# Forgetting attention: reciprocal roots on GpSimd for two units at a time, the output product in mid-slot, one spreading transfer for both heads

## What is computed

```python
q, k, v = x @ Wq, silu_conv(x @ Wk), silu_conv(x @ Wv)      # 16 heads of 64, conv of 4 taps
q = q / sqrt(mean(q**2, head) + 1e-6) * qnw                 # k likewise, with knw
cum = cumsum(log_sigmoid(x @ Wf + bf))
attn = softmax(causal(q @ k.T / 8 + cum[t] - cum[s]))
out = attn @ v
out = out / sqrt(mean(out**2, head) + 1e-6) * onw * silu(x @ Wg)
return out @ Wo
```

## Time and profile before

| | us |
|---|---|
| median of 3 runs (lowest, highest) | 2411.89 (2408.7, 2413.06) |
| the profiled execution | 2409.0 |
| its span | 2407.1 |
| `forget_units`, from the first instruction of its own to the last | 908.7 to 1955.5 |

### The profile page before, as it was taken

How to read it: one execution, slowest core, us unless ns; L and a number is a source line. 1 busy time by engine, 2 the same in 40 slices (tenths; PEclk the granted TensorE clock), 3 DMA queues, 4 the chain that set the end, 5 groups by cost and what they waited for, 6 DMA issues and landing times. The chain is left out here.

```text
span 2407.1 us, 35881 instructions
## 1 busy us (share of the span) xinstructions
PE 1917.6 (80%) x11731; PEld 872.8 (36%) x11731; DVE 1613.6 (67%) x2361; ACT 1396.5 (58%) x2254; POOL 919.5 (38%) x746
## 2 busy tenths in 40 slices
PE   5448886377775755899999999999999957599997
PEld 2113331343453422344444444444444413222222
DVE  5979995686447856778888888888886436711112
ACT  2446662333333334577777777777775533389995
POOL 0156663244014511345545555555555422700001
PEclk8779998588896977899999999999999988799999
DMA  2000000000000010111111111112111100411120
GB/s 89 0 13 0 0 0 0 1 1 1 0 1 0 1 38 24 39 58 57 57 57 57 57 57 57 56 59 57 57 57 58 46 19 18 114 40 48 46 53 36
DMA packets 66143, 86.12 MB, mean 36 GB/s; under 512 B 13344, under 2 KB 37216, under 8 KB 65888
## 3 DMA queue, kind: packets, MB, share of 16 engines
q1 hardware_dynamic: 60944, 81.37, 11.4%
q10 hardware_dynamic: 5040, 2.72, 0.4%
HBM read 72.12 MB, written 11.93 MB: 35 GB/s over the span
## 5 line engine op out<-in xcount | busy, mean ns | idle before, releaser
L2001 ACT ACTIVATE rt_p<-rt_ps_s 128x1024 f32<-128x1024 f32 x256 | 240.3, 1040 | 32.8 <-PE rt_ps_o L1946 17.4
L1634 DVE SCALAR_TENSOR_TENSOR fu_kv<-fu_ps_kv,fa_vec,fu_kv 128x511 f32<-128x511 f32 x366 | 252.6, 738 | 6.4 <-ACT fu_kv L1542 5.5
L1706 POOL TENSOR_TENSOR fu_p<-fu_p 128x768 f32<-128x768 f32 x64 | 116.7, 1823 | 260.2 <-PE fu_ps_n L1392 255.8
L1362 PE MATMUL fu_ps_s<-fu_qn,fu_kn 64*128 64x512 f32 (+3 forms) x1024 | 190.8, 470 | 7.4 <-ACT fu_p L1529 5.6
L601 POOL TENSOR_TENSOR scan_hC<-scan_h,scan_c 128x1024 f32<-128x1024 f32 x64 | 150.7, 2355 | 84.4 <-DVE scan_h L581 84.4
L1392 PE MATMUL fu_ps_n<-fu_p,fu_vt 128*64 128x512 f32 (+3 forms) x1024 | 166.0, 445 | 0.0
L526 PE MATMUL scan_ps_y<-scan_hC,w_ident 128*128 128x512 f32 x256 | 132.1, 640 | 40.9 <-POOL scan_hC L601 24.3
L581 DVE TENSOR_TENSOR_SCAN scan_h<-scan_dA,scan_ps_b 128x1024 f32<-128x1024 f32 x64 | 146.4, 2287 | 2.2
L1717 POOL TENSOR_TENSOR fu_num<-fu_num,fu_sg 128x512 f32<-128x512 f32 x64 | 81.3, 1270 | 172.3 <-DVE fu_sg L1667 172.3
L1946 PE MATMUL rt_ps_o<-rt_p,rt_va 128*32 128x512 f32 x1024 | 138.1, 611 | 10.0 <-ACT rt_p L2001 8.1
L1420 PE MATMUL fu_ps_kv<-w_XN,fa_wp 128*128 128x512 f32 x244 | 126.6, 643 | 16.7 <-DVE fu_cr L1599 15.3
(11 more groups left out here) (349 smaller groups left out, 4942.4 us busy)
## 6 DMA issues: line engine op xcount, KB each, us to landing
fu_rb<-rms_rows SPq DMA_DIRECT2D x256, 128.0 KB, 2.9
fu_ro<-rms_rows SPq DMA_DIRECT2D x128, 128.0 KB, 3.0
ra_stackq<-rope_parts SPq DMA_DIRECT2D x168, 32.0 KB
ra_stackk<-rope_parts SPq DMA_DIRECT2D x168, 32.0 KB
rope_parts<-rp_q SPq DMA_DIRECT2D x24, 128.0 KB, 2.0
rope_parts<-rp_k SPq DMA_DIRECT2D x24, 128.0 KB, 2.0
rms_rows<-fu_r SPq DMA_DIRECT2D x14, 192.0 KB, 2.1
w_X<-in_xT SPq DMA_DIRECT2D x4, 512.0 KB
```

Source lines behind the costliest of these rows:

```text
L1362: pe.matmul(sps[:, h, at:at + T - t * P], k[head(h), t * P:(t + 1) * P], q[head(h), t * P:T], start=(at == 0), stop=False)
L1634: dve.scalar_tensor_tensor(acc, projected(a, k)[:, 0:T - j], vec[:, a % GA, at:at + 1], acc, ALU.mult, ALU.add).then_inc(done, 1)
L1706: pool.tensor_tensor(tail, tail, P13[:, :, 0:3 * P], ALU.add).then_inc(s.d1, 1)
L2001: act.activation(pr[k % 2][i][:, :, :], sps[(U * n + u) % RING][:, :, :], ACT.Exp, scale=DH_B ** -0.5).then_inc(s.exp, 1)
```

## The change

WIN is 2: each second slot (i % 2 == 1) is a root slot. AHEAD is still 8, OUT is 4 (each unit's output a slot earlier; `o` is i - 5, so that odd o, with the output projection, falls into even slots, and never into a root slot). In a root slot ACT now adds epsilon for queries and keys (an Identity with bias, 64 x 512) in DVE's place, and squares; DVE adds for the output (1633 in the new numbering). The two function table loads, Ln and Exp are gone. In their place SP folds the mean squares, 4 rows of 512 for each of the three kinds, into 32 partitions x 64 (`VAR`, up to four small transfers), DVE makes a first guess of 1/sqrt by integer arithmetic on the bits (1663), and GpSimd refines it with eleven instructions on 96 x 64, each waiting for the one before (1731 to 1752), between its sums of probabilities and the gating of `fu_num`. The write of the roots to DRAM stands in the next, even slot.

The output product moves from the start of DVE's slot to behind the last tap, ahead of the last reduction. The spread is one transfer over 128 partitions in place of two over 64: `rows.rearrange("h (o t) -> h o t").broadcast_to([2, 64, T])`, with outermost count 2, then 64 with step 0.

```diff
-WIN = 4
+WIN = 2
+ROOT_SCALE = 1.8348544414191587e-20
...
-    OUT = WIN + 1
+    OUT = WIN + 2
...
+        def spread(rows):
+
+            return rows.rearrange("h (o t) -> h o t", o=1).broadcast_to([2, 64, T])
... (SP)
                         for j in range(2):
-                            for h in range(2):
-                                row = 32 * j + 2 * (u % WIN) + h
-                                sp.dma_start(RB[head(h), j, :], rows_dram[u // WIN, row:row + 1, :].broadcast_to([64, T])).then_inc(s.rb, 16)
+                            row = ROWS * j + 2 * (u % WIN)
+                            sp.dma_start(RB[:, j, :], spread(roots_dram[u // WIN, row:row + 2, :])).then_inc(s.rb, 16)
...
+                    if i % WIN == 1 and windows(i - 1) != (None, None):
...
+                        sp.wait_ge(s.msq, min(j + 1, U // WIN))
+                        sp.wait_ge(s.mso, max(j - 3, 0))
+                        for g in range(3):
+                            if g < 2 and r.start == 0:
+                                sp.dma_start(VAR[32 * g:32 * g + 32, :], MS[32 * g:32 * g + ROWS, :]).then_inc(s.fold, 16)
...
                         sp.wait_ge(s.og, u)
-                        for h in range(2):
-                            row = 64 + 16 * h + u % WIN
-                            sp.dma_start(RO[head(h), :], rows_dram[u // WIN + 2, row:row + 1, :].broadcast_to([64, T])).then_inc(s.ro, 16)
+                        row = 2 * ROWS + u % WIN
+                        sp.dma_start(RO[:, :], spread(roots_dram[u // WIN + 4, row:row + WIN + 1:WIN, :])).then_inc(s.ro, 16)
... (ACT)
+                        act.activation(MS[0:64, :], ssps[0:64, :], ACT.Identity, bias=w.eps_rms[0:64, 0:1]).then_inc(s.msq, 1)
...
-                        act.preload_act_table_set("natural_log_exp_and_others")
...
-                        act.activation(MS[r, :], MS[r, :], ACT.Ln).then_inc(s.ln, 1)
...
-                        act.activation(R[j % 2][r, :], MS[r, :], ACT.Exp, scale=-0.5).then_inc(s.r, 1)
... (DVE)
-                        dve.tensor_scalar(MS[0:64, :], ssps[0:64, :], RMS_EPS, None, ALU.add).then_inc(s.msq, 1)
...
+                        dve.tensor_scalar(ROOT[r, :].bitcast(I32), VAR[r, :].bitcast(I32), 1, 0x7fffffff, ALU.logical_shift_right, ALU.bitwise_xor).then_inc(s.bits, 1)
... (GpSimd, eleven such steps)
+                        pool.wait_ge(s.bits, j + 1)
+                        pool.tensor_scalar(y, y, ROOT_SCALE, None, ALU.mult).then_inc(s.ya, 1)
...
+                        pool.tensor_tensor(R[j % 2][r, :], y, f, ALU.mult).then_inc(s.r, 1)
```

More of the change, by code:

```diff
@@ L1288, in forget_units @@
         MS = st.sb("ms", [96, T])
-        R = [st.sb(f"r{k}", [96, T]) for k in range(2)]
+        VAR, ROOT, STEP1, STEP2 = (st.sb(n, [96, CUT]) for n in ("var", "root", "step1", "step2"))
+        R = [st.sb(f"r{k}", [96, CUT]) for k in range(2)]
         kvps, sps, mps = (st.ps(n, [P, 2, T]) for n in ("kv", "s", "m"))
         nps, ssps = st.ps("n", [P, T]), st.ps("ss", [P, T])
-        s = st.sems("set ones kvp tap t1 t2 cv th sk sv vt vc qp qc q2 k2 sa so dsq msq mso ln r rb ro put cr0 cr1 cr2 qn kn qm km "
+        s = st.sems("set ones kvp tap t1 t2 cv th sk sv vt vc qp qc q2 k2 sa so dsq msq mso fold bits ya yb yc yd y1 ye yf yg yh yi r rb ro put cr0 cr1 cr2 qn kn qm km "
                     "mx red hi ml rt rr sc ex pv d1 d2 ds n2 nc gp tg sg gated og wo x")
@@ L1612, in _ @@
                     if real(u):
-                        dve.wait_ge(s.rb, 64 * (u + 1))
+                        dve.wait_ge(s.rb, 32 * (u + 1))
                         dve.wait_ge(s.set, 9)
@@ L1713, in _ @@
                         pool.tensor_tensor(tail, tail, P13[:, :, 3 * P:T], ALU.add).then_inc(s.ds, 1)
+                    q, o = windows(i - 1) if i % WIN == 1 else (None, None)
+                    if q is not None or o is not None:
+                        j, r = (i - 1) // WIN + 3, slice(0, rows_of(q, o).stop)
+                        x, y, e, f = VAR[r, :], ROOT[r, :], STEP1[r, :], STEP2[r, :]
+                        pool.wait_ge(s.bits, j + 1)
+                        pool.tensor_scalar(y, y, ROOT_SCALE, None, ALU.mult).then_inc(s.ya, 1)
+                        pool.wait_ge(s.ya, j + 1)
+                        pool.tensor_tensor(e, y, y, ALU.mult).then_inc(s.yb, 1)
+                        pool.wait_ge(s.yb, j + 1)
+                        pool.tensor_tensor(e, e, x, ALU.mult).then_inc(s.yc, 1)
+                        pool.wait_ge(s.yc, j + 1)
+                        pool.tensor_scalar(e, e, -0.5, 1.5, ALU.mult, ALU.add).then_inc(s.yd, 1)
+                        pool.wait_ge(s.yd, j + 1)
+                        pool.tensor_tensor(y, y, e, ALU.mult).then_inc(s.y1, 1)
+                        pool.wait_ge(s.y1, j + 1)
+                        pool.tensor_tensor(e, y, y, ALU.mult).then_inc(s.ye, 1)
+                        pool.wait_ge(s.ye, j + 1)
+                        pool.tensor_tensor(e, e, x, ALU.mult).then_inc(s.yf, 1)
+                        pool.wait_ge(s.yf, j + 1)
+                        pool.tensor_scalar(f, e, 0.375, -1.25, ALU.mult, ALU.add).then_inc(s.yg, 1)
+                        pool.wait_ge(s.yg, j + 1)
+                        pool.tensor_tensor(f, f, e, ALU.mult).then_inc(s.yh, 1)
+                        pool.wait_ge(s.yh, j + 1)
+                        pool.tensor_scalar(f, f, 1.875, None, ALU.add).then_inc(s.yi, 1)
+                        pool.wait_ge(s.yi, j + 1)
+                        pool.wait_ge(s.put, 16 * max(j - 1, 0))
+                        pool.tensor_tensor(R[j % 2][r, :], y, f, ALU.mult).then_inc(s.r, 1)
                     if real(c):
```

76 lines of the change are left out of this document (39 added, 37 removed).

## The result

The changed kernel takes 3080.35 us (median of 4 runs, 3076.26 to 3084.05), the kernel before 2411.85 beside it: a ratio of 1.277, 95% interval 1.275 to 1.280, slower by 668.5 us. The forecast was 3100 in a range of 2850 to 3450. The profiled execution has a span of 3075.6. Of all executions behind this document two took far longer than the others of their kernel and are left out of every ratio, 4632.5 us in `base_ogmid_ro2` and 2540.0 in a run of the kernel before.

A forecast was written before the change was run, and what follows sets the result against it. PE bounds the kernel before (80% busy); after the change, a circle through two-engine spreads. 56 slots +668, head +21, end +4: +693 on the profiled 2409.0, forecast 3100 us, range 2850 to 3450.

The forecast's parts named there:

- The spread: two engines: RB and RO transfers, source outermost count 2: dealt out to one DMA engine per head, two of 16.
- The price: Rows on two engines at 0.086 us each: RB 11.0, RO 5.5, together 16.5 us a slot, plus 2.4 fixed.
- the fixed part: Latency of a spread transfer beyond its rows' time: 2.4 us, counted once per circle.
- The circle: Loop QN, taps, output product, SP, RO, RB, next QN: 26.8 us, 27.5 in odd slots, 3.95 less without taps.
- 56 slots: Stretch from the eighth QN to the last: 1500 us in place of 832.7, +668.
- The head: Before the eighth QN: seven intervals of 15.3 us, first QN some 4 later, one RB pushed back some 4; +21.
- The end: Last root takes three more steps but the last slot is gone: +4 us, between -5 and +15.
- What it does else: Roots, folds, GpSimd instructions, moved addition and product: all covered in a 27 us circle, priced only for the rivals.
- the first rival: New spread uses all 16 engines, landing as before in 2.9 us; product and late maxima cost: 2413 us, chance 0.06.
- the second rival: All 16 engines, and the output product runs free of GpSimd's sum: 2392 us, faster, chance 0.06.
- price none, up to 0.5 where KN meets QN: GpSimd's eleven root instructions, some 4.5 us every second slot: no cost, or up to 0.5 us.
- What would show it: Signs: fu_rb landing 11 us or more, fu_ro 7, slots of 27, QN and KN idle over 10, PE 60%, DMA 2/16.

The follow-up runs named there:

- base_ogmid_ro2: The kernel before the change with only the output product moved to mid-slot and two buffers for RO: 2418.11 us, ratio 1.0036.
- two: The changed kernel with only the old spread put back (two transfers of 64 partitions, 64 outermost on both sides): 2438.60 us, ratio 1.0119.
- two_ro2: The changed kernel with the old spread put back and two buffers for RO, so SP need not wait for the same slot's product: 2426.53 us, ratio 1.0069.
- pair: The changed kernel with 64 outermost again, each head's query and key rows in one transfer, two issues for RB: 2429.83 us, ratio 1.0083.

## Why the prediction was right

- **The spread: two engines.** Right. 0.15 of 16 engines are busy at 52 GB/s, and 4 and 8 on the source's outermost dimension give rates and times in between, with 64 on the other side. The rule of the Trainium skill (DMA: Bandwidth & Descriptors, "Why a DMA increments its semaphore by 16 and not by 1") agrees: the largest number up to 16 that divides both sizes is 2, 4 and 8 in these kernels. The smaller of the two sizes would be the same here; no run tells them apart.
- **The price.** A row was taken at 0.086, from 16 engines at work at once, and comes to 0.079 where two work alone; the fixed part was taken at 2.4 and is then 18.38 - 192 x 0.079 = 3.2. The two errors go against each other: together 18.4 (18.0 in the slot ahead) for 18.9.
- **The circle.** Right in all its pieces. From QN to the product's end, in a slot with the addition, 8.51 was forecast (1.78 + 0.72 + 1.98 + 1.19 + 1.97 + 0.87) and 8.49 is measured (1.89 + 0.72 + 1.98 + 1.19 + 1.97 + 0.74); then 0.07 for 0.07. That the parts fit to 0.02 is partly luck: QN to the instruction behind it took longer (1.89 for 1.78) and the product less (0.74 for 0.87). A pair is 52.7 (1744.28 to 1796.94) for 54.3. With two engines and this circle opened 2798 are left of 3080.
- **56 slots.** From the eighth QN to the last 1462.2 us for 1500, +629.5 for +668: RO's and RB's way was priced 0.5 to 0.9 a slot too high. The head and the end, both dearer than forecast, give 14 of these 38 us back, so the total is off by less than its largest part is.
- **The head.** The first QN is 4.2 later for 4, the eighth, below, 28.6 for 21: of the seven intervals ahead of it two are 17.8 and two 19 for the 15.3 of the sum, the others 14.7 to 15.0. The trace shows what stands ahead of RB in SP's queue there. In the interval from 995.88 to 1013.68 SP issues the gate's rows only at 1000.65, 2.9 after QN's end, when PE's scores let it, and RB behind them; the other of 17.8 is the same. In the first of 19 four folds stand ahead, and in the second RO's rows, which the sum had at 4. The end: +10.4 for +4, in the bounds. Timeline, the gate's rows and RB on SP's queue, and the eighth QN:

```profile
1000.65 0.55 SPq L1344 DMA_DIRECT2D fu_cr<-ncum_rows  x2
1001.32 1.05 SPq L1350 DMA_DIRECT2D fu_rb<-rms_rows  x2
...
1084.20 1.86 DVE L1627 SCALAR_TENSOR_TENSOR fu_qn<-fu_qs,fu_qw,fu_rb 128x512 f32<-128x512 f32 x1 [3.27 <-DMA fu_rb<-rms_rows]
```

- **What it does else.** "In a circle of 27 us all of this is covered" was not tried by itself, but nothing in the 52.7 of a pair speaks against it. The costs that I gave for the rivals were too low. `two`, with the landing of the first rival, is not at 2413 but at 2439, and with the circle opened besides (`two_ro2`, where the product takes 0.74, nearly the second rival's condition) the kernel is not at 2392 but at 2427. Two steps in the rivals' sums failed. "From about 12 engines the spread (2.8 us on each) lands in time again": the circle through the product is there with the old spread too, at 14.8 us, with 4.7 of SP's issues in it, and opening it gives 12 us. (Fewer issues alone do not open it, as `pair` shows.) And "price none, up to 0.5 where KN meets QN": the maximum is 0.99 late in every second slot, and ACT's squares make the addition 0.7 late in the other.
- **What would show it.** Slots of 26 to 27 and 32 GB/s in the stretch are as listed. Others came weaker than listed: QN is idle for 8.4 us in the mean and KN for 10.6, for "over 10", PE is busy for 67% of the span and not 60%, and the DMA share is 0.09 over a pair and 0.15 only while rows move, for 2/16. The landing of `fu_rb` and `fu_ro` is not given by the profile for the new shape; from RB's issue at 1780.05 to QN 16.9 us pass, with RO's rows ahead of RB's.

## What to carry to other kernels

Before two transfers are merged into one, look at the outermost count of both sides, the source of a broadcast above all: `[2, 64, T]` moves the same bytes as two `[64, T]`, at 52 GB/s where those came to 159 in a short window. If issues are to be saved, merging along an inner dimension, as `pair` does, keeps 64 outermost and lost no time here; it won none in the circle either, since the larger transfers landed later by what their issues saved. And when a step moves later in an engine's order, follow who waits for it on the queues: here the product's place closed a circle through SP that cost more (54 of 64 us in the kernel before) than the product's own time, and a second buffer opened it.
